# A two-layer graph network on one core: LN2's row sums and centred squares in place of bn_stats, the scale of x one group further ahead, W_O transposed between the halves of group 0's mix

## Chip, cores and metric

One core of one Trainium2 chip runs the whole program. The metric is device time in microseconds (us) of one execution; the kernel before takes 594.0 us, median of 3 runs (593.91 to 594.22). Lower is better.

## The reference

x is 128 batches of 64 nodes with 512 features; adj is one 64 x 64 matrix of zeros and ones. What is computed, cut to what matters:

```python
# layer 0
W = adj * adj
x = layernorm(x + einsum('bnf,nm->bmf', x, W) + bias)          # LN1
# layer 1
z_l = x @ W_lang.T;  z_g = x @ W_grav.T;  v = x @ W_V.T
A_l = maximum(zn @ zn.T, 0) * not_eye                          # zn: rows of z_l at norm 1
A_g = exp(-d2(z_g) / (2 * sigma**2)) * not_eye
K = w_l * rownorm(A_l * adj) + (1 - w_l) * rownorm(A_g * adj)
x = layernorm(x + (K @ v) @ W_O.T)                             # LN2
```

## The kernel before

All 128 batches are cut into 16 groups of 8. A group is 512 rows, held as 4 pairs of 128 rows (two batches each) by 512 features. There is one instruction stream for each engine, in an order written out by hand; semaphores alone tie the engines together. Float32 values enter most products as a high and a low float16 part (`h_hi`, `h_lo` and so on), three matmuls for one product. The high part is a copy on ScalarE, the low part a subtraction on VectorE, or on GpSimd for x and for two pairs of h.

`iteration(g, ...)` does, for group g, all of layer 1 up to its similarities; for `before` (g-1) the rest of layer 1 and LN2; for `nxt` (g+1) layer 0 and LN1; for `split` (g+2) the scaling of x and its split into halves. The order on TensorE in the middle of the run:

- `mix(nxt, 0)` (L420) is layer 0 for half of nxt's pairs. Its start is used below as the mark at which an iteration begins.
- `project(g, 0..3)`, then `mix(nxt, 1)`, `project(g, 4)`, `x_norm(split)` (L426, one small matmul that sums the squares of x), `kernel_t(before)` (L528), `project(g, 5)`, `attend(before, 0)` (L548), `project(g, 6)`, `attend(before, 1)`, `project(g, 7)`. The projections (L449) are 12, 9, 6, 3 matmuls of 512 columns, twice. `project(g, 0)` waits for the transposed h (`ht_hi`, `ht_lo`: eight DMA transposes per group from SyncE's queue, L345) and for `ulo_ready` of the group before, that is for `u_low` 0 and 1; `project(g, 2)` for `u_low` 3; `project(g, 3)` for `p_low(g, 0)`, `project(g, 4)` for `p_low(g, 1)`.
- `values(g, 0)`, `gram(g)` (L481), `values(g, 1..3)` (L467), `spread` (L496) and `symmetrise` (L505, L507), and the next mark.

The chain that leads to `spread`, over four engines: `gram` -> `t_copy` (ScalarE) -> `t_diagonal` (GpSimd, L1343) -> `diagonals`, `squared_norms` (VectorE) -> `inverse_norm` (GpSimd, a power, L1349, makes `rr`) -> `diagonal_matrices` (VectorE, L960, makes `r_sb`) -> `spread`. After `symmetrise`: `rectify`, `exponent` (ScalarE), `similarities`, `gravities`, `row_sums` and so on (VectorE) -> `ks_sb` -> `kernel_t`.

LN2 of the group before: `residual` (L1011, VectorE) adds h to the product and writes `o`; `out_stats` (L1016) is one bn_stats for each pair; `out_moments` (L1020, L1022) aggregates; `ln2` on GpSimd adds epsilon and takes the power -1/2; `out_shift` (L1026) makes -mean * rstd in `nmr2`; `normalise` (L748, ScalarE) scales each pair; one DMA stores the group (L323).

x of a group needs one scale (a power of the sum of its squares): `x_squares` (L686) -> `x_sum` -> `x_norm` -> `x_base` -> `x_scale` and `x_back` (GpSimd) -> `x_inverse`; `x_scaled` (L691) applies it, `x_high` (L697) and `x_low` (L1316, GpSimd) split. All of it is done for `split` in one iteration, but for the squares, which are taken one iteration earlier.

Before the iterations: products of ones that keep TensorE busy (`keep_warm`, L403), the Gram product of W_lang (L633), layer 0 of group 0 in two halves (L420), sixteen transposes of W_O (L657) into `front`, the Gram product of W_grav (L633), which needs the banks that ScalarE has copied out, and M = W_V.T W_O.T (L668), which for each bank needs `g_copied`, VectorE's copy of the W_grav product. VectorE's order there: bias, statistics, norm and low half of group 0 (`first_bias` to `h_low`, L926), then the `g_copied` copies. In iteration 0 `m_low` (L1051) makes the low half of M, which `values(g, 0)` waits for, chunk by chunk.

## Time and profile before

| | |
|---|---|
| median of 3 runs | 594.0 us |
| the profiled execution | 594.79 us, span of its instructions 593.0 us |
| mean granted TensorE clock | 0.996 |
| busy: TensorE matmul, VectorE, ScalarE, GpSimd | 96%, 88%, 60%, 38% of the span |
| chain that ended last, by engine | TensorE 67%, VectorE 11%, GpSimd 7% |

The span runs from the first instruction's start to the last one's end. Matmuls are pipelined: the row of a 512-column float16 matmul lasts 0.38 us, and the next starts 0.216 us later when nothing holds it. A busy share of 96% can therefore hide short stalls; starts are to be compared, not only the idle times in brackets.

### The profile page before, as it was taken

The numbers are of one execution on the slowest core, as the hardware profiler recorded it, in microseconds if no ns is written. First come the engines' busy times: TensorE is split into PE (matmuls) and PEld (weight loads), VectorE is DVE, ScalarE is ACT, GpSimd is POOL, SyncE is SP. The second block draws the span as 40 slices with busy tenths as digits, with TensorE's granted clock in tenths as the row PEclk, the third lists the DMA queues.
The fourth block names the chain that finished last, engine by engine and source line by source line (L and its number), as shares of the span: only waits on it lengthen the run. The fifth ranks groups of instructions, "written<-read, shape, count | busy, mean of one in ns | idle before, by whom it ended". The sixth has DMA issues, their size and how long they took to land.

```text
span 593.0 us, 14867 instructions
## 1 busy us (share of the span) xinstructions
PE 566.6 (96%) x5743; PEld 285.0 (48%) x5743; DVE 519.6 (88%) x1027; ACT 358.4 (60%) x670; POOL 223.1 (38%) x230
## 2 busy tenths in 40 slices
PE   9899899999999999999999999999999999899993
PEld 6544545445354545445454545445454545446451
DVE  1767789998999999999999999999999999997765
ACT  2576645757566675857666675857666675634532
POOL 0141524535162533526162533526162533514021
PEclk9999999999999999999999999999999999999998
DMA  9853241344525142343525142343525130314103
GB/s 253 219 116 72 45 99 20 93 105 72 141 60 152 36 130 59 72 128 71 141 60 153 35 130 59 71 129 71 141 59 154 35 107 12 68 64 74 71 2 143
DMA packets 89659, 55.21 MB, mean 93 GB/s; under 512 B 71072, under 2 KB 71072, under 8 KB 89632
## 3 DMA queue, kind: packets, MB, share of 16 engines
q1 hardware_dynamic: 89632, 54.84, 37.4%
q8 instruction: 18, 0.29, 0.2%
q14 instruction: 9, 0.07, 0.1%
HBM read 21.27 MB, written 16.78 MB: 64 GB/s over the span
## 4 chain that ended last, share of the span: by engine, by line
PE 67%; DVE 11%; POOL 7%; issue 6%; ACT 4%; SPq 2%; DMA 1%; DVEq 0%; POOLq 0%; ACTq 0%
PE proj L449 30%; PE proj L467 12%; PE front L420 3%; PE ps_t L481 3%; DVE h L921 3%; POOL h_lo L1321 3%; PE ps_v L496 3%; POOL rr L1349 3%; SPq L345 2%; PE ps_t L505 2%; PE ps_k L548 2%; PE proj L633 2%; PE front L548 2%; PE proj L668 2%; DVE p_lo L941 2%
## 5 line engine op out<-in xcount | busy, mean ns | idle before, releaser
L1316 POOL TENSOR_TENSOR x_lo<-x_in,x_hi 128x512 f16<-128x512 f32 x60 | 72.5, 1219 | 104.6 <-ACT x_hi L697 104.6
L707 ACT ACTIVATE p_hi<-proj 128x512 f16<-128x512 f32 x128 | 75.5, 592 | 51.8 <-PE proj L449 51.3
L467 PE MATMUL proj<-m_hi,ht_hi 128*64 128x512 f16 x512 | 98.6, 382 | 0.0
L467 PE MATMUL proj<-m_hi,ht_lo 128*64 128x512 f16 x512 | 97.9, 379 | 0.0
L467 PE MATMUL proj<-m_lo,ht_hi 128*64 128x512 f16 x512 | 97.9, 379 | 0.0
L941 DVE TENSOR_TENSOR p_lo<-proj,p_hi 128x512 f16<-128x512 f32 x128 | 85.4, 678 | 4.5 <-ACT p_hi L707 4.4
L701 ACT ACTIVATE h_hi<-h 128x512 f16<-128x512 f32 x64 | 39.9, 630 | 43.4 <-DVE h L921 43.4
L1300 POOL TENSOR_TENSOR ve<-mv,eps_ln 128x4 f32<-128x4 f32 x31 | 6.2, 201 | 158.1 <-DVE mv L914 142.0
L449 PE MATMUL proj<-ht_hi,l_lang_hi 128*128 128x512 f16 x160 | 60.9, 381 | 2.7 <-DMA ht_lo<-h_lo 1.3
L449 PE MATMUL proj<-ht_hi,l_grav_hi 128*128 128x512 f16 x160 | 61.3, 383 | 0.1
L449 PE MATMUL proj<-ht_hi,l_lang_lo 128*128 128x512 f16 x160 | 60.6, 379 | 0.0
L449 PE MATMUL proj<-ht_hi,l_grav_lo 128*128 128x512 f16 x160 | 60.6, 379 | 0.0
L449 PE MATMUL proj<-ht_lo,l_lang_hi 128*128 128x512 f16 x160 | 60.6, 379 | 0.0
L449 PE MATMUL proj<-ht_lo,l_grav_hi 128*128 128x512 f16 x160 | 60.6, 379 | 0.0
L712 ACT ACTIVATE uv<-proj 128x512 f16<-128x512 f32 x64 | 37.7, 590 | 34.1 <-PE proj L467 34.1
L921 DVE TENSOR_SCALAR h<-y,mv,rstd 128x512 f32<-128x512 f32 x64 | 55.9, 896 | 1.4 <-POOL rstd L1304 1.4
L1321 POOL TENSOR_TENSOR h_lo<-h,h_hi 128x512 f16<-128x512 f32 x30 | 40.7, 1357 | 34.1 <-ACT h_hi L701 34.1
L481 PEld LDWEIGHTS ps_t<-ht_hi,p_hi 128*128 128x128 f16 x512 | 44.8, 98 | 9.4 <-issue 6.9
L1349 POOL TENSOR_TENSOR rr<-nsq,minus_half 64x8 f32<-64x8 f32 x16 | 34.2, 2136 | 39.6 <-DVE nsq L951 39.4
L481 PE MATMUL ps_t<-ht_hi,p_hi 128*128 128x64 f16 x512 | 46.6, 193 | 2.4 <-DVE p_lo L941 2.1
L481 PE MATMUL ps_t<-ht_lo,p_hi 128*128 128x64 f16 x512 | 46.5, 193 | 0.0
L481 PE MATMUL ps_t<-ht_hi,p_lo 128*128 128x64 f16 x512 | 46.5, 193 | 0.0
(210 smaller groups left out, 1319.2 us busy)
## 6 DMA issues: line engine op xcount, KB each, us to landing
x_in<-in_x SPq DMA_DIRECT2D x32, 512.0 KB, 6.3
out<-o SPq DMA_DIRECT2D x15, 1024.0 KB, 4.9
w_raw_lang<-in_L_gnn_W_lang SPq DMA_DIRECT2D x4, 256.0 KB, 3.6
o<-in_L_gnn_W_O SPq DMA_DIRECT2D x1, 1024.0 KB, 10.9
w_raw_grav<-in_L_gnn_W_grav SPq DMA_DIRECT2D x4, 256.0 KB, 11.2
uv<-in_L_gnn_W_V SPq DMA_DIRECT2D x1, 1024.0 KB, 16.2
ht_hi<-h_hi SPq DMA_TRANSPOSE x64, 2.5
ht_lo<-h_lo SPq DMA_TRANSPOSE x64, 2.5
```

The lines of the kernel that those rows point to most:

```text
L449: mm = pe.matmul(proj[j % 3][:, :], a[s][:, blk(k, c), :], b[g.parity][:, k, :], start=(n == 0), stop=(n == len(passes) - 1))
L467: mm = pe.matmul(proj[j % 3][q * N:(q + 1) * N, :], a[g.parity][:, k, rows:rows + N], b[:, k, :], start=(n == 0), stop=(n == len(passes) - 1))
L481: mm = pe.matmul(ps_t[:, b * N:(b + 1) * N], a[:, c, b, :, :].rearrange("p s n -> p (s n)"), t[g.parity][:, c, b * N:(b + 1) * N], start=( ...
L548: mm = pe.matmul(banks[2 * a + q][side * N:(side + 1) * N, :], kt[half, 2 * a + side, :], u[half, 2 * a + side, :], start=(n == 0 and 2 * ...
L701: act.activation(h_hi[:, p, :], h[g.parity][:, p, :], ACT.Copy).then_inc(hhi_ready, 1)
L707: act.activation(p_hi[:, j % 4, :, j // 4, :], by_batch(proj[j % 3]), ACT.Copy).then_inc(phi_ready, 1)
L712: act.activation(u_hi[:, p, :], proj[(8 + p) % 3][:, :], ACT.Copy).then_inc(uhi_ready, 1)
L921: dve.tensor_scalar(h[g.parity][:, p, :], y[:, p, :], mv1[:, p, 0:1], rstd1[:, p:p + 1], ALU.subtract, ALU.mult).then_inc(h_ready, 1)
L941: dve.tensor_tensor(p_lo[:, j % 4, :, j // 4, :], by_batch(proj[j % 3]), p_hi[:, j % 4, :, j // 4, :], ALU.subtract).then_inc(plo_ready, 1)
L1316: pool.tensor_tensor(x_lo[:, p, :], x_in[g.parity][:, p, :], x_hi[:, p, :], ALU.subtract).then_inc(xlo_ready, 1)
L1321: pool.tensor_tensor(h_lo[:, p, :], h[g.parity][:, p, :], h_hi[:, p, :], ALU.subtract).then_inc(hlo_ready_pool, 1)
L1349: pool.tensor_tensor(rr[L, :], nsq[L, :], minus_half[L, :], ALU.pow).then_inc(rr_ready, 1)
```

## The change

LN2 of all groups but the last no longer uses bn_stats. `residual` gives the row sums too, `out_means` turns them into -mean/sqrt(512), and ScalarE's `o_squares` takes ((o - mean)/sqrt(512)) squared with its own sum as the variance. `out_shift` moves ahead of `u_low` 1 and 2 on VectorE, `normalise(before, 0)` ahead of `rectify` on ScalarE, and `u_high(g, 3)` behind `exponent`.

The squares of x, its sum, `x_norm`, `x_base`, `x_scale`, `x_back` and `x_inverse` are now for `third` (g+3), so that the scale of `split` is known when an iteration starts; its scaling and halves move to the front of the iteration. `xscale` gets two buffers. In iteration 0 the whole of both is done: `split` and then `third`.

`mix(nxt, 1)` moves from behind `project(g, 3)` to behind `project(g, 2)`. On GpSimd `t_diagonal` goes ahead of `h_low(nxt, 2)` and `inverse_norm` ahead of `h_low(nxt, 3)`. W_O's transposes go between the two halves of group 0's mix and into `weight_bank`. `WARM_START` goes from 5 to 10.

```diff
-WARM_START = 5
+WARM_START = 10
...
+                         in1=h[g.parity][:, p, :], op0=ALU.mult, op1=ALU.add,
+                         accum_out=osum[:, p:p + 1]).then_inc(sum_ready, 1)
-            def out_stats(g, p): ...
-            def out_moments(g): ...
+            def out_means(g, half):
+                pairs = slice(2 * half, 2 * half + 2)
+                dve.wait_ge(sum_ready, g.count(4, 2 * half + 2))
+                dve.tensor_scalar(omean[:, pairs], osum[:, pairs], -(D ** -1.5), None, ALU.mult).then_inc(omean_ready, 1)
...
+            def o_squares(g, p):
+                act.wait_ge(omean_ready, g.count(2, p // 2 + 1))
+                act.activation(o_square[:, p, :], o[:, p, :], ACT.Square, scale=D ** -0.5, bias=omean[:, p:p + 1],
+                               accum_out=ovar[:, p:p + 1]).then_inc(ovar_ready, 1)
...
             def ln2(g):
-                inverse_std(g, mv2_ready, mv2, ve2_ready, ve2, rstd2_ready, rstd2)
+                pool.wait_ge(ovar_ready, g.count(4, 4))
+                pool.tensor_tensor(ve2[:, :], ovar[:, :], eps_ln[:, :], ALU.add).then_inc(ve2_ready, 1)
+                pool.wait_ge(ve2_ready, g.count(1, 1))
+                pool.tensor_tensor(rstd2[:, :], ve2[:, :], minus_half[:, 0:PAIRS], ALU.pow).then_inc(rstd2_ready, 1)
```

The new order on each engine, from the values on (TensorE: `x_norm(third)` after `values(g, 1)`):

```
ScalarE, iterations with a group before and a third:
  p_high 0, x_scaled(split) 0 1, p_high 1, p_high 2, ks_high, x_high(split) 0, p_high 3, x_scaled(split) 2 3,
  kt_high, p_high 4, x_high(split) 1 2, p_high 5, x_squares(third) 0 1, p_high 6, p_high 7, x_squares(third) 2 3,
  h_high 0 1 2, o_squares 0, t_copy, x_high(split) 3, o_squares 1, u_high 0, h_high 3, o_squares 2, u_high 1,
  o_squares 3, u_high 2, normalise 0, rectify, exponent, u_high 3, normalise 1 2 3
VectorE, from p_low 5: residual 2, p_low 6, residual 3, p_low 7, out_means 0, norm_rows 0 1 2, h_low 0,
  out_means 1, x_sum(third), h_low 1, norm_rows 3, diagonals, squared_norms, x_base(third), u_low 0, shifted,
  diagonal_matrices, out_shift, u_low 1, u_low 2, x_inverse(third), similarities, gravities, add_bias 0, u_low 3
GpSimd: x_low(split) 0, ln1 with x_low(split) 1 inside, t_diagonal, h_low 2, inverse_norm, h_low 3,
  x_scale(third), x_back(third), ln2(before), x_low(split) 2 3
ScalarE, iteration 0: p_high 0, x_squares(split) 0 1, p_high 1, x_squares(split) 2 3, p_high 2, m_high 0, p_high 3,
  m_high 1, p_high 4, x_scaled(split) 0 1 2 3, p_high 5, x_squares(third) 0 1, p_high 6, p_high 7,
  x_high(split) 0 1 2, x_squares(third) 2 3, h_high 0 1 2, t_copy, ...
VectorE, iteration 0: add_bias 0, row_stats 0, add_bias 1, p_low 0, m_scale, x_sum(split), row_stats 1, p_low 1, ...
  x_base(split), row_stats 3, p_low 4, ... p_low 7, norm_rows 0 1 2, h_low 0, m_low 0 1 2 3, ...
```

```diff
             mix(Group(0, 0), 0, first=True)
+            pe.wait_ge(o_moved, 16)
+            for c in range(DC):
+                pe.wait_ge(l_copied, c + 1)
+                for e in range(DC):
+                    mm = pe.transpose(weight_bank[c][:, e * P:(e + 1) * P],
+                                      w_raw["o"][:, e, c * P:(c + 1) * P], ident[:, :])
+                mm.then_inc(wot_done, 1)
             pe.wait_ge(wssq_ready, 1)
...
             mix(Group(0, 0), 1, first=True)
-            pe.wait_ge(o_moved, 16)
-            for c in range(DC):
-                ...
-            pe.wait_ge(l_copied, DC)
             gram_of("grav")
```

## Rows read from the trace of the kernel before

**Rows 1.** Waits of TensorE, whole span: us in total, times, longest.

```profile
PE ps_v L496 <- DVE r_sb L960: 4.5, 8, 0.6
PE ps_v L496 <- issue: 3.0, 7, 0.5
...
PE proj L449 <- DMA ht_lo<-h_lo: 1.3, 2, 0.9
```

**Rows 2.** Timeline of TensorE at the marks: start us, length us, idle in brackets.

```profile
78.02 0.41 PE L420 MATMUL front<-x_hi,wmix_hi 64*64 64x512 f16 x4
...
279.60 0.41 PE L420 MATMUL front<-x_hi,wmix_hi 64*64 64x512 f16 x4
...
312.89 0.41 PE L420 MATMUL front<-x_hi,wmix_hi 64*64 64x512 f16 x4
...
513.25 0.41 PE L420 MATMUL front<-x_hi,wmix_hi 64*64 64x512 f16 x4
```

**Rows 3.** Timeline of TensorE inside the iteration that starts at 279.60.

```profile
285.99 0.38 PE L449 MATMUL proj<-ht_hi,l_lang_lo 128*128 128x512 f16 x1
286.40 0.39 PE L449 MATMUL proj<-ht_hi,l_lang_hi 128*128 128x512 f16 x1
...
299.14 0.38 PE L467 MATMUL proj<-m_hi,ht_lo 128*64 128x512 f16 x2
299.45 0.20 PE L481 MATMUL ps_t<-ht_hi,p_hi 128*128 128x64 f16 x1
...
309.93 0.38 PE L467 MATMUL proj<-m_hi,ht_lo 128*64 128x512 f16 x2
310.78 0.67 PE L496 MATMUL ps_v<-r_sb,w_spread 128*128 128x512 f32 x1 [0.47 <-issue]
```

**Rows 4.** Timeline of GpSimd, same iteration.

```profile
303.70 1.46 POOL L1343 TENSOR_TENSOR t_diag<-t_sb,eye 128x512 f32<-128x512 f32 x1
...
307.83 2.13 POOL L1349 TENSOR_TENSOR rr<-nsq,minus_half 64x8 f32<-64x8 f32 x1 [1.11 <-DVE nsq L951]
...
311.39 1.01 POOL L1304 TENSOR_TENSOR rstd<-ve,minus_half 128x4 f32<-128x4 f32 x1
```

**Rows 5.** Timeline of VectorE, same iteration: p_low 1 and the matrix for spread.

```profile
287.06 0.68 DVE L941 TENSOR_TENSOR p_lo<-proj,p_hi 128x512 f16<-128x512 f32 x1
...
310.00 0.68 DVE L960 TENSOR_TENSOR r_sb<-eye,rr 64x512 f32<-64x512 f32 x1 [0.80 <-POOL rr L1349]
```

**Rows 6.** Instructions on tile nmr: duration ns min/median/max, first and last start.

```profile
L1026 DVE SCALAR_TENSOR_TENSOR nmr<-mv,rstd x15: 154/1109/1117, 111.3 to 574.0; 128x4 f32<-128x4 f32 x15
```

**Rows 7.** Groups of instructions by line and form: busy us, mean ns | idle.

```profile
L686 ACT ACTIVATE x_square<-x_in 128x512 bf16<-128x512 f32 x60 | 37.1, 620 | 0.8 <-DMA x_in<-in_x 0.8
...
L686 ACT ACTIVATION_READ_ACCUMULATOR x_square<-x_in 128x1 f32 x60 | 11.6, 193 | 0.0
```

**Rows 8.** Timeline of TensorE before iteration 0 and at its gram.

```profile
17.04 1.09 PE L420 MATMUL front<-x_in,wmix 64*64 64x512 f32 x8
19.03 1.16 PE L657 MATMUL front<-ident,o 128*128 128x128 f32 x8 [0.91 <-DVE y L885]
...
30.01 3.60 PE L668 MATMUL proj<-wo_t,uv 128*128 128x512 f32 x8
...
62.25 0.19 PE L481 MATMUL ps_t<-ht_hi,p_hi 128*128 128x64 f16 x1 [2.10 <-DVE p_lo L941]
```

**Rows 9.** Timeline of SyncE's queue: the load of W_O.

```profile
5.84 0.43 SPq L354 DMA_DIRECT2D o<-in_L_gnn_W_O  x1
```

**Rows 10.** DMA issues by line: KB each, median us to landing.

```profile
o<-in_L_gnn_W_O SPq DMA_DIRECT2D x1, 1024.0 KB, 10.9
```

**Rows 11.** Timeline of VectorE before and in iteration 0.

```profile
25.63 2.50 DVE L926 TENSOR_TENSOR h_lo<-h,h_hi 128x512 f16<-128x512 f32 x4
...
63.23 3.63 DVE L1051 SCALAR_TENSOR_TENSOR m_lo<-m_f,up,m_hi 128x512 f16<-128x512 f32 x4
```

**Rows 12.** Timeline of ScalarE in iteration 0: two x_scaled.

```profile
58.97 1.33 ACT L691 ACTIVATE x_in<-x_in,xscale 128x512 f32<-128x512 f32 x2
```

More of the change, by code:

```diff
@@ L486, in gram, with spread @@
                 mm.then_inc(gram_done, 1)
-            def spread(g, first, split):
-                if split:
-                    pe.wait_ge(xbase_ready, split.prev().count(1, 1))
+            def spread(g, first, third):
+                if third:
+                    pe.wait_ge(xbase_ready, third.prev().count(1, 1))
                 pe.wait_ge(shifted_ready, g.count(1, 1))
@@ L574, in iteration @@
                 split = nxt.next() if has_split else None
+                third = split.next() if has_square else None
                 if has_next:
@@ L578, in iteration @@
                     mix(nxt, 0)
+                project(g, 0, first)
                 if first:
@@ L611, in iteration @@
                 if has_next:
+                    if has_square:
+                        pe.wait_ge(xsum_ready, third.prev().count(1, 1))
+                        if first:
+                            pe.wait_ge(xbase_ready, 2)
+                        x_norm(third)
                     values(g, 2)
                     values(g, 3)
-                    spread(g, first, split)
+                    spread(g, first, third)
                     symmetrise(g, split)
@@ L766, in iteration @@
                 split = nxt.next() if has_split else None
-                square = split.next() if has_square else None
-                if first:
-                    m_high(0)
+                third = split.next() if has_square else None
                 p_high(g, 0, first)
@@ L772, in iteration @@
                     x_squares(split, 0)
-                    m_high(1)
+                    x_squares(split, 1)
+                elif has_split:
+                    x_scaled(split, 0)
+                    x_scaled(split, 1)
                 p_high(g, 1, first)
-                if first:
-                    x_squares(split, 1)
-                p_high(g, 2, first)
                 if first:
@@ L1104, in iteration @@
                 split = nxt.next() if has_split else None
+                third = split.next() if has_square else None
+                if has_prev:
+                    gravities(before)
                 if has_next:
                     add_bias(nxt, 0)
-                if has_split and not first:
-                    x_sum(split)
                 if has_prev:
-                    gravities(before)
                     u_low(before, 3)
@@ L1123, in iteration @@
                 p_low(g, 0)
+                if first:
+                    m_scale()
+                    x_sum(split)
                 if has_prev:
@@ L1133, in iteration @@
                 p_low(g, 2)
-                if first:
-                    x_sum(split)
                 if has_next:
@@ L1159, in iteration @@
                     residual(before, 2, False)
+                p_low(g, 6)
+                if has_prev:
                     residual(before, 3, False)
-                p_low(g, 6)
                 p_low(g, 7)
+                if has_prev:
+                    out_means(before, 0)
                 if has_next:
                     norm_rows(nxt, 0, before)
+                    norm_rows(nxt, 1, before)
+                    norm_rows(nxt, 2, before)
+                    h_low(nxt, 0)
                 if first:
@@ L1301, in inverse_std @@
                 if between:
-                    x_scale(between)
+                    x_low(between, 1)
                 pool.wait_ge(ve_ready, g.count(1, 1))
@@ L1357, in iteration @@
                 split = g.next().next() if has_split else None
-                if has_next:
-                    ln1(nxt, split)
-                if has_split:
+                third = split.next() if has_square else None
+                if first:
+                    x_scale(split)
+                    x_back(split)
+                    ln1(nxt)
                     x_low(split, 0)
                     x_low(split, 1)
-                    x_back(split)
+                else:
+                    if has_split:
+                        x_low(split, 0)
+                    if has_next:
+                        ln1(nxt, split)
                 if has_next:
+                    t_diagonal(g)
                     h_low(nxt, 2)
-                    t_diagonal(g)
+                inverse_norm(g)
+                if has_next:
                     h_low(nxt, 3)
-                inverse_norm(g)
+                if has_square:
+                    x_scale(third)
+                    x_back(third)
                 if has_prev:
```

174 lines of the change are left out of this document (86 added, 88 removed).

## The prediction

> **What bounds the kernel now.** I read the table of busy shares first: TensorE is busy in 96% of the span, so an edit counts only by what it does to TensorE's idle time. The view of its waits comes next. The reader is to see that one stall repeats: `spread` waits for `r_sb`, named as the matrix itself or as "issue", 15 times and 7.5 us in all; the transposed h was late twice, for 1.3 us [rows 1]. Third come the marks, the starts of `mix(nxt, 0)`. From the first (78.02) to the fourteenth (513.25) are 13 periods, 33.48 us on average; one of the middle is 33.29 [rows 2]. TensorE's timeline inside it shows what the list of waits hides: its rows overlap, so that only starts tell. From the last matmul of the values to `spread` are 0.85 us, where the same kind of change of stage, values to `gram`, takes 0.31: a stall of 0.54. And within `project(g, 3)` one step takes 0.41 where 0.216 is the rule: another 0.2, for `p_low 0` [rows 3]. So a period has a floor of about 33.48 - 0.9 = 32.6; the 0.9 is 0.54 to 0.68 at `spread` (7.5 us of waits over 15, and some 0.1 of overlap each), 0.2 at the projection and the rest of the first three periods, where the transposes and `p_low` were later still.
>
> **Part 1: LN2 and the reordered tail.** VectorE loses four bn_stats (0.68 each, 0.60 from start to start) and four aggregations, and gains two tiny multiplications and the sums of the four residuals. No VectorE row shows what such a sum costs. Bounds: 0, or 0.1 a residual, which is what ScalarE's read of its accumulator adds between starts (its row of 193 ns overlaps the one before [rows 7]). I take 0.07, as for the smallest VectorE instructions; 0.3 a group. VectorE still gains some 2 us a group between `p_low 7` and `diagonals`. ScalarE gains four squares of about 0.71 from start to start (620 ns and its read [rows 7]), 2.9 us. It is busy 60% of the time, so its sum hides them; where they stand matters, below.
>
> The chain to `spread`: let Γ be the start of `gram` (299.45 [rows 3]). Before, `t_diagonal` started at Γ+4.25 behind `h_low 2`, and `inverse_norm` at Γ+8.4, held by VectorE, which was busy with statistics and `u_low 0` [rows 4]. After: `t_copy` ends at Γ+3.6 (a `gram` of 2.9, 0.1, a copy of 0.6), `t_diagonal` takes 1.46 [rows 4] and `h_low 2` 1.16, to Γ+6.2, when `diagonals` and `squared_norms` (0.95) are done as well. The power takes 2.13 [rows 4], to Γ+8.35, and `diagonal_matrices` 0.68 [rows 5], to Γ+9.05, or Γ+10.1 if it is held by `h_low 3`, which GpSimd starts at the same moment. `spread` could start at Γ+10.5 (309.93 + 0.31 - 299.45 [rows 3]) plus 0.03 for the moved `x_norm`. It no longer waits: 0.6 a period. Before, its end was 2.11 us ahead of the next mark (310.78 to 312.89 [rows 2, 3]), so the new mark is at Γ+12.95.
>
> What is late next is LN2's own chain, which the change puts in front of things that TensorE needs. GpSimd after the power: `h_low 3` to Γ+9.55, `x_scale` and `x_back` to about Γ+10.3, the addition to Γ+10.6, rstd 1.01 [rows 4] to Γ+11.6. The squares of ScalarE are done by then: the last follows the values' second part at about Γ+7.9. `out_shift` waits for rstd, and `u_low 1`, `u_low 2` and `similarities` are queued behind it; `normalise 0` waits for `out_shift`, and `rectify`, `exponent` and `u_high 3` are queued behind that.
>
> How long `out_shift` takes is the disputed price: its fifteen rows have a median of 1109 ns and a minimum of 154, on four columns [rows 6]. The long ones stand beside an `x_low` of GpSimd, the short one beside an idle GpSimd. After the change it again meets `x_low 2`, which starts as rstd ends. So 1.1, to Γ+12.7; 0.15 is the other end. The Trainium skill (SBUF — State Buffer, Who interferes with whom) states that a VectorE instruction with two SBUF inputs contends with a GpSimd instruction that reads SBUF, and that whoever is first keeps the shared pair to its end. By that rule `out_shift` always waits for the whole `x_low`, and the row's median agrees.
>
> From Γ+12.7 on: `u_low 1` ends at Γ+13.4, and `project(nxt, 0)` wants it at Γ+12.95+0.77 = Γ+13.7: 0.3 to spare. `normalise 0` takes 0.71, `rectify` 0.62 and `similarities` starts at Γ+14.2, 1.25 after the mark, where it was at 0.74 before. From there to the end of `p_low 1` stand in VectorE's queue, as starts: 0.7 similarities, 0.7 gravities, 0.65 bias, 0.6 `u_low 3`, 0.6 row sums, 0.6 statistics, 0.07, 0.65 bias, 0.15 clamp, 0.6 `p_low 0`, 0.1, 0.55 statistics, 0.15, 0.68 `p_low 1`: 6.8 us, to 8.05 after the mark (before it ended at 8.14: 287.06 + 0.68 - 279.60 [rows 2, 5]). `mix(nxt, 1)` now stands ahead of `project(g, 3)`, so `p_low 0`, at 6.65, is in time for 7.4, and the 0.2 there goes. `project(g, 4)` wants `p_low 1` at 8.03 and gets it some 0.1 late. So the period is 32.6 + 0.1; as this chain has no slack, each 0.1 more on GpSimd or ScalarE is 0.1 on the period. Bounds: 32.6 (`out_shift` at 0.15), and 33.1 (0.4 more, if `h_low 3` and `x_back` are held up by VectorE). I take 32.75. Thirteen periods: 13 x (33.48 - 32.75) = 9.5 us saved; between 4.9 and 11.4.
>
> **Part 2: the scale of x two groups ahead.** The same instructions as before, moved. GpSimd gets two `x_low` out of the way of the `norm_rows` (the tile's halves are ready earlier), the transposes of h start over 1 us earlier, and the 0.9 us that TensorE waited for them in group 14 goes [rows 1]. x of `third` is loaded when it is squared: SyncE's queue order stays, and a load is out well before `p_high 5`. In iteration 15, without mixes, `normalise 1` to `3` now hold `p_high 0` back; I charge 0.5. Tail together: -0.4.
>
> **Part 3: iteration 0.** Here both groups' x work is done at once. TensorE reaches `project(g, 0)` at about 45.7 (part 4; 46.1 before). ScalarE has four squares of `split` before `p_high 2`, and `x_sum(split)` now stands before `p_low 1` on VectorE: it waits for the last square at about 52.8, `p_low 1` ends at 54.2, and `project(g, 4)`, due at 53.4, starts at 54.3. Then `x_norm`, `x_base` and `x_scale` give the scale at 57.9, and ScalarE has four `x_scaled` (1.33 for two [rows 12], 2.5 for four) before `p_high 5` and two squares (1.4) before `p_high 6` and `7`, to 63.4; `p_low 7` ends at 64.2. `gram` starts at 64.3 instead of 62.25 [rows 8]: 2.05 lost. Then three `x_high` and two squares stand before `h_high 0` (66.9), which `h_low 0` waits for, and only behind that come the four `m_low`, 3.63 us before [rows 11]: 67.6 to about 71.2. `values(g, 0)`, due at 67.2, runs at their pace and ends at 71.9 instead of 69.8; if `t_diagonal` does not hold them up, 1.1 earlier. Lost: 1.1 to 2.1; I take 1.65. The whole: 3.7 us lost; bounds 2 and 5.
>
> **Part 4: the start.** W_O is issued at 5.84 and lands 10.9 us later, at 16.75 [rows 9, 10]. The sixteen transposes, now ahead of the second half of the mix, take about 2.3 [rows 8] from there, and the mix goes from 17.04 to about 19.35. The five further products of ones take 0.43 each and half of that is lost anyway to later work at the low clock level; they end before W_O lands, so they are hidden. VectorE's chain behind the second half moves by 2.3: its `h_low` end at 30.4 instead of 28.13 [rows 11], the first `g_copied` is at 30.8, and M starts at 30.85 instead of 30.01 [rows 8]. TensorE alone would have been ready 1.0 earlier, since 2.2 us of its waits are gone, but VectorE decides. Then M is 0.84 late, and the matmul of norms, which TensorE waited for before `project(g, 0)`, now stands behind it: 1.2 back. Net -0.4, in part 3 already.
>
> **The sum.** Against the profiled execution's 594.79 (span 593.0 and 1.8 around it): -9.5 - 0.4 + 3.7 = -6.2, so 588.6. The median of the runs is 0.8 below the profiled one: 594.0 - 6.2 = 587.8.
>
> **Rivals.** Differences within 0.2% (1.2 us) can't be told from none here.
> - *The tail chain is shorter.* `out_shift` gets through before `x_low`, or ScalarE's queue is a little faster: the period is at its floor of 32.6, and iteration 0 loses only 2 to 3. 594.0 - 11.4 - 0.4 + 2.5 = 584.7. For it speaks the 154 ns row, against it the fourteen long ones [rows 6]. Chance 0.22.
> - *The tail chain is longer.* GpSimd's small instructions are held by VectorE's: the period is 33.0 to 33.2. Then 594.0 - 5 - 0.4 + 3.7 = 592.3. Chance 0.15; a part of it counts as no change.
> - *Slower.* The one mechanism: `normalise 0` and `out_shift` wait for rstd in two in-order queues. Where rstd comes 0.6 us later than at Γ+11.6, `u_low 1` stops `project(nxt, 0)` and `p_low 1` stops `project(g, 4)`; the period is 33.35 and saves 1.7, less than iteration 0 costs: 596. It decides from a period of 33.2 on. By the Trainium skill's rule named above the price of each meeting of `h_low 3` with `diagonal_matrices` and of `x_low 2` with `out_shift` is a whole instruction; both are in the sum once, and this would need them on GpSimd's side as well. Chance 0.11.
> - *The change of statistics does nothing by itself*, since VectorE is not what TensorE waits for: then only the order counts. The sum above already says so in part: the bn_stats matter only ahead of `diagonals`. It gives the same time.
>
> The forecast itself has 0.52: periods of 32.65 to 32.95 and a loss of 3 to 4.5. Faster by over 0.2%: 0.52 + 0.22 + most of 0.15, 0.82; within 0.2%: 0.07; slower: 0.11. The range from the bounds: 13 x 0.9 and a loss of 1 to 2 give 583; a period of 33.1 and a loss of 4 give 592.7. I give 582.5 to 593.2.
>
> **What would show it right or wrong.** Marks 32.7 to 32.8 apart; `spread` 0.31 behind the last matmul of the values; a step above 0.216 before `project(g, 4)`; `out_shift` about 1.1 long and starting as rstd ends; `gram` of group 0 at 64.3, its `values(g, 0)` stretched to 4.5 us, the second mark near 81.7; M at 30.85. It is wrong if residuals with a sum take well over 0.82, if the long idle before the first `gram` (3.3 us, 2.10 before [rows 8]) is followed by matmuls at half speed, or if a store or load is late.

## The result: 589.3 us, 0.8% faster, and the profile after

Six runs of the changed kernel have a median of 589.29 us (588.82 to 589.98), six of the kernel before beside them 594.11 (593.11 to 595.71): ratio 0.9918, 95% interval 0.9903 to 0.9933. The profiled executions took 588.82 (span 587.0) and 594.79 (span 593.0). So the span lost 6.0 us where the medians lost 4.8: the profiled run of before lies 0.7 above its median, that of after 0.5 below.

The marks, from TensorE's timeline; they answer to [rows 2]:

```profile
43.73 0.41 PE L426 MATMUL front<-x_hi,wmix_hi 64*64 64x512 f16 x4
...
80.67 0.41 PE L426 MATMUL front<-x_hi,wmix_hi 64*64 64x512 f16 x4
...
277.57 0.41 PE L426 MATMUL front<-x_hi,wmix_hi 64*64 64x512 f16 x4
...
310.38 0.41 PE L426 MATMUL front<-x_hi,wmix_hi 64*64 64x512 f16 x4
...
507.05 0.41 PE L426 MATMUL front<-x_hi,wmix_hi 64*64 64x512 f16 x4
```

The period is 32.82 (310.38 - 277.57 is 32.81; before 33.29 there and 33.48 in the mean); the last of the thirteen, whose iteration has no third group and so no `x_norm`, is 32.58. From the second mark to the last 435.23 became 426.38: 8.85 saved. The second mark came 2.65 later (78.02 to 80.67): lost. From the last mark to the end of the span 79.75 became 79.95: 0.2 lost. 8.85 - 2.65 - 0.2 = 6.0, the difference of the spans.

The waits of TensorE, longest first (us in total, times, longest), against [rows 1]:

```profile
PE ps_t L487 <- DVE p_lo L970: 3.6, 2, 3.3
PE proj L676 <- DVE l_grav_f L1269: 1.5, 1, 1.5
PE proj L455 <- DMA ht_lo<-h_lo: 1.4, 2, 0.8
...
PE proj L473 <- DVE m_lo L1077: 0.6, 1, 0.6
PE proj L662 <- DMA o<-in_L_gnn_W_O: 0.5, 1, 0.5
```

`spread` is gone from the list. All that is left is at the start, in iteration 0 and in the last two iterations. Inside a period, TensorE's timeline around the moved `x_norm` (L432) and at `spread` (L502):

```profile
302.52 0.38 PE L473 MATMUL proj<-m_hi,ht_lo 128*64 128x512 f16 x2
302.84 0.18 PE L432 MATMUL ps_v<-xsum,ones 128*128 128x1 bf16 x1
302.94 0.41 PE L473 MATMUL proj<-m_hi,ht_hi 128*64 128x512 f16 x2
...
307.93 0.38 PE L473 MATMUL proj<-m_hi,ht_lo 128*64 128x512 f16 x2
308.25 1.13 PE L502 MATMUL ps_v<-r_sb,w_spread 128*128 128x512 f32 x2
```

`spread` starts 0.32 behind the last matmul of the values, where it was 0.85 [rows 3]. But from 302.52 to 302.94 are 0.42 where values follow each other every 0.216: `x_norm` costs 0.2 here. The power that `spread` hangs on, on GpSimd:

```profile
303.40 1.63 POOL L1375 TENSOR_TENSOR rr<-nsq,minus_half 64x8 f32<-64x8 f32 x1
```

It starts 6.2 behind the start of `gram` (297.22), where it was 8.4 [rows 3, 4], and takes 1.63 where it took 2.13.

LN2's chain, VectorE's timeline of the same iteration:

```profile
308.69 1.11 DVE L1052 SCALAR_TENSOR_TENSOR nmr<-omean,rstd 128x4 f32<-128x4 f32 x1 [1.96 <-POOL rstd L1354]
309.72 1.27 DVE L960 TENSOR_TENSOR uv<-proj,uv 128x512 f16<-128x512 f32 x2
...
311.16 0.68 DVE L996 TENSOR_TENSOR a_sb<-e_sb,ps_v 64x512 f32<-64x512 f32 x1
```

`out_shift` starts as rstd ends (308.65) and takes 1.11, as predicted; `u_low 1` ends at 310.4, 0.76 before `project(nxt, 0)` at 311.16; `similarities` starts 0.78 after the mark.

Iteration 0, TensorE at the gram of group 0 and in `values(g, 0)`, and the clock beside it (windows: length; busy time of each engine with its instructions in brackets; granted clock; DMA share; GB/s):

```profile
62.63 0.19 PE L487 MATMUL ps_t<-ht_hi,p_hi 128*128 128x64 f16 x1 [3.32 <-DVE p_lo L970]
...
68.77 0.38 PE L473 MATMUL proj<-m_hi,ht_lo 128*64 128x512 f16 x2
69.76 0.41 PE L473 MATMUL proj<-m_hi,ht_hi 128*64 128x512 f16 x2 [0.61 <-DVE m_lo L1077]
```

```profile
62.60:64.00 1.40, 1.37 (x42) 1.40 (x43) 1.40 (x2) 1.40 (x5) 1.40 (x2) 0.88 0.00 0
64.00:65.00 1.00, 1.00 (x23) 1.00 (x21) 1.00 (x2) 0.95 (x3) 0.70 (x1) 0.50 0.00 0
...
67.00:68.00 1.00, 1.00 (x12) 0.57 (x12) 1.00 (x3) 0.88 (x2) 0.20 (x1) 0.96 0.52 105
```

After 3.32 us of idle time and about 1 us of work the granted clock fell to 0.50, its level of 1.2 GHz, for some 3 us; gram lasted 4.38 (62.63 to 67.01) instead of 2.89. Then the last quarter of `values(g, 0)` waited for the fourth `m_low`.

### The profile page after: what moved, and what is told of

The parts are those of the page before. It is cut to its first block, busy times and chain, and to the rows that moved or that the text cites. A ratio compares the mean times of both kernels' runs of the same rounds, so it can differ in the third digit from the quotient of the medians.

```text
span 587.0 us, 14987 instructions
## 1 busy us (share of the span) xinstructions
PE 568.2 (97%) x5753; PEld 287.3 (49%) x5753; DVE 461.1 (79%) x982; ACT 396.0 (67%) x790; POOL 214.6 (37%) x230
## 4 chain that ended last, share of the span: by engine, by line
PE 85%; DVE 6%; SPq 3%; DMA 3%; ACT 2%; POOL 1%; issue 1%; POOLq 0%; DVEq 0%; ACTq 0%
PE proj L455 35%; PE proj L473 26%; PE ps_t L487 7%; PE front L426 4%; PE ps_v L502 3%; PE ps_t L511 2%; PE ps_k L552 2%; PE front L552 2%; SPq L351 2%; PE proj L676 2%; DMA o<-in_L_gnn_W_O 2%; DMA ht_lo<-h_lo 1%; PE ps_v L532 1%; DVE p_lo L970 1%; DVE h L950 1%
## 5 line engine op out<-in xcount | busy, mean ns | idle before, releaser
L1339 POOL TENSOR_TENSOR x_lo<-x_in,x_hi 128x512 f16<-128x512 f32 x60 | 76.1, 1280 | 124.4 <-ACT x_hi L705 124.4
L970 DVE TENSOR_TENSOR p_lo<-proj,p_hi 128x512 f16<-128x512 f32 x128 | 87.5, 685 | 7.2 <-ACT p_hi L715 5.6
L761 ACT ACTIVATE o<-o,nmr,rstd 128x512 f32<-128x512 f32 x60 | 45.7, 807 | 47.3 <-DVE nmr L1052 46.9
L1369 POOL TENSOR_TENSOR t_diag<-t_sb,eye 128x512 f32<-128x512 f32 x15 | 19.2, 1281 | 103.5 <-ACT t_sb L726 103.5
L487 PE MATMUL ps_t<-ht_hi,p_hi 128*128 128x64 f16 x512 | 48.1, 195 | 3.6 <-DVE p_lo L970 3.6
L487 PEld LDWEIGHTS ps_t<-ht_hi,p_hi 128*128 128x128 f16 x512 | 45.7, 99 | 10.7 <-issue 6.9
L709 ACT ACTIVATE h_hi<-h 128x512 f16<-128x512 f32 x64 | 36.8, 622 | 18.5 <-DVE h L950 18.4
L487 PE MATMUL ps_t<-ht_hi,p_lo 128*128 128x64 f16 x512 | 48.0, 195 | 0.0
L487 PE MATMUL ps_t<-ht_lo,p_hi 128*128 128x64 f16 x512 | 48.0, 195 | 0.0
L487 PEld LDWEIGHTS ps_t<-ht_lo,p_hi 128*128 128x128 f16 x512 | 45.9, 99 | 0.0
L487 PEld LDWEIGHTS ps_t<-ht_hi,p_lo 128*128 128x128 f16 x512 | 45.9, 99 | 0.0
```

Source lines behind the costliest of these rows:

```text
L487: mm = pe.matmul(ps_t[:, b * N:(b + 1) * N], a[:, c, b, :, :].rearrange("p s n -> p (s n)"), t[g.parity][:, c, b * N:(b + 1) * N], start=( ...
L709: act.activation(h_hi[:, p, :], h[g.parity][:, p, :], ACT.Copy).then_inc(hhi_ready, 1)
L761: act.activation(o[:, p, :], o[:, p, :], ACT.Identity, scale=rstd2[:, p:p + 1], bias=nmr2[:, p:p + 1]).then_inc(out_ready, 1)
L970: dve.tensor_tensor(p_lo[:, j % 4, :, j // 4, :], by_batch(proj[j % 3]), p_hi[:, j % 4, :, j // 4, :], ALU.subtract).then_inc(plo_ready, 1)
L1339: pool.tensor_tensor(x_lo[:, p, :], x_in[g.parity][:, p, :], x_hi[:, p, :], ALU.subtract).then_inc(xlo_ready, 1)
L1369: pool.tensor_tensor(by_batch(t_diag), by_batch(t_sb), over_batches(eye2), ALU.mult).then_inc(tdiag_ready, 1)
```

## Experiments

Each time is to be read beside the 594 us of the kernel before, which was run with it; ratios carry their 95% intervals. Edits are against the changed kernel unless said.

### Which half of the change carries the gain: old_statistics, only_statistics

`old_statistics` keeps every new order and puts LN2's bn_stats back, into a place where VectorE was idle:

```diff
-                    out_means(before, 0) ... out_means(before, 1)
                     h_low(nxt, 1)
                     norm_rows(nxt, 3, before)
+                    for p in range(PAIRS): out_stats(before, p)
...
                 shifted(g)
+                    out_moments(before)
```

> The changed kernel with LN2's bn_stats, aggregation and shift as before (statistics in VectorE's idle stretch of 2.5 us behind the fourth norm_rows), all the new orders kept. Theory 1, that the orders carry the gain and the bn_stats only mattered where they stood: the period stays at 32.82, spread 0.31 behind the last matmul of the values, and the time is 589.3, within 0.7 of the changed kernel's. Theory 2, that VectorE's relief carries it: diagonals come 2 us later, spread stalls again by 0.5 or more, period 33.3 to 33.5, time 594 to 597.

589.17 us, ratio 0.9911 (0.9889 to 0.9933): the changed kernel's time, and theory 1. VectorE's timeline shows the four bn_stats in the idle stretch:

```profile
298.85 2.46 DVE L1035 BATCH_NORM_STATS2 stats<-o 128x6 f32<-128x512 f32 x4
301.58 0.69 DVE L966 TENSOR_REDUCE diag<-t_diag 128x8 f32<-128x512 f32 x1 [0.26 <-POOL t_diag L1360]
```

The period is 32.81 with the old statistics (marks at 276.93 and 309.74 in TensorE's timeline). `only_statistics` is the reverse: the kernel before, with LN2's sums and squares and nothing else (squares on ScalarE ahead of and behind `t_copy`, and around `u_high 1`).

> The kernel before with only LN2's statistics changed (sums in the residual, squares on ScalarE), every order as before. Theory 1, that the four bn_stats and aggregations held diagonals back: diagonals run as t_diagonal ends, the power starts at 7 instead of 8.4 us behind the start of gram, spread waits no more, the period falls by 0.6 to 32.9 and the time to about 586, as iteration 0 loses nothing. Theory 2, that the new orders are what is needed (GpSimd's h_low ahead of the power): the stall at spread stays above 0.3, time 592 to 594.

591.47 us (586.55 to 592.51, wider than any other), ratio 0.9930 (0.9904 to 0.9957). The time is neither theory's, but the steady period is about what theory 1 said (32.9):

```profile
278.15 0.41 PE L426 MATMUL front<-x_hi,wmix_hi 64*64 64x512 f16 x4
...
284.55 0.38 PE L455 MATMUL proj<-ht_hi,l_lang_lo 128*128 128x512 f16 x1
284.96 0.39 PE L455 MATMUL proj<-ht_hi,l_lang_hi 128*128 128x512 f16 x1
...
310.94 0.41 PE L426 MATMUL front<-x_hi,wmix_hi 64*64 64x512 f16 x4
```

32.79: `spread` waits no more (308.81, 0.32 behind the values' last at 308.49); `diagonals` runs as `t_diagonal` ends and the power starts 7.2 behind the start of `gram` (305.22 - 298.01), not 8.4. The step of 0.41 for `p_low 0`, which the old place of `mix(nxt, 1)` leaves, is still there; the new orders remove that 0.2, but their place for `x_norm` costs as much, so that both halves come to the same period. What spoils the time lies outside. The first three periods are 33.2 to 33.7, the fifth 33.1, and the transposed h is late at both ends of the run (view of waits: 4.6 us, four times, against 1.4 in the changed kernel). The longest such wait (2.50) was followed by a low clock, as was the idle time before the gram of group 0:

```profile
62.10:66.60 4.50, 4.49 (x98) 4.45 (x100) 4.50 (x5) 0.69 (x2) 2.68 (x3) 0.62 0.14 29
...
541.00:543.00 2.00, 0.00 (x0) 0.00 (x0) 1.73 (x3) 1.95 (x4) 0.00 (x0) 1.00 0.00 0
543.00:545.00 2.00, 1.96 (x7) 0.83 (x8) 1.26 (x4) 1.84 (x3) 0.00 (x0) 0.70 0.00 0
```

The ten runs differ with their mean granted clock: the four longest (592.24 to 592.51, the profiled one among them) had 0.986 or 0.987, the two shortest (586.55 and 587.21) 0.996 and 0.995. At that higher clock the statistics alone, in the old orders, are faster than the whole change.

So each half of the change alone removes the stall at `spread`: the new statistics free VectorE ahead of `diagonals`, the new orders let the chain start sooner on GpSimd and find VectorE idle. Done both, the second adds nothing to the period.

### Iteration 0: first_scalar_only, first_both, first_filler

`first_scalar_only` mends ScalarE's order in iteration 0:

```diff
                 if first:
-                    for p in range(PAIRS):
-                        x_scaled(split, p)
+                    x_scaled(split, 0)
+                    x_scaled(split, 1)
                 p_high(g, 5, first)
-                x_squares(third, 0); x_squares(third, 1)
+                x_scaled(split, 2)
                 p_high(g, 6, first)
                 p_high(g, 7, first)
+                x_scaled(split, 3)
                 x_high(split, 0) ... x_high(split, 2)
-                x_squares(third, 2); x_squares(third, 3)
+                x_squares(third, 0) ... x_squares(third, 3)
```

> The changed kernel with ScalarE's order of iteration 0 mended alone: two x_scaled ahead of p_high 5, one behind it, the fourth and all squares of third behind p_high 7. Theory 1, that in iteration 0 two things are late, the products' high halves and then m_low: gram of group 0 starts at about 60.7 instead of 62.63 and keeps the full clock, but the fourth m_low still ends at 69.2 or later, so the second mark moves by 0.5 at most (80.2 to 80.7) and the time is 589. Theory 2, that the late gram and the clock behind it are what iteration 0 lost: the second mark moves by 2 to 3.5 and the time is 586 to 587.

589.25 us, ratio 0.9917 (0.9890 to 0.9943). Theory 1 was right on what decides, but the second mark, at 81.51, is 0.8 beyond its range.

```profile
60.76 0.19 PE L487 MATMUL ps_t<-ht_hi,p_hi 128*128 128x64 f16 x1 [1.50 <-DVE p_lo L977]
...
66.56 0.41 PE L473 MATMUL proj<-m_hi,ht_hi 128*64 128x512 f16 x2 [2.84 <-DVE m_lo L1084]
```

```profile
65.05 0.69 DVE L962 TENSOR_TENSOR h_lo<-h,h_hi 128x512 f16<-128x512 f32 x1 [2.24 <-ACT h_hi L709]
65.66 4.65 DVE L1084 SCALAR_TENSOR_TENSOR m_lo<-m_f,up,m_hi 128x512 f16<-128x512 f32 x4
```

The gram came 1.9 earlier, at full clock, and TensorE then stood idle for 2.84 before `m_low`. The four `m_low` took 4.65 instead of 3.75: the earlier gram brought GpSimd's `t_diagonal` and `h_low 2` forward, from 67.80 to 66.62, so that they ran beside all of the last three. In the profile of `no_x_norm` (below), where `t_diagonal` came only at 69.23, the four took 2.73. The Trainium skill (SBUF — State Buffer, Who interferes with whom) states that a VectorE instruction with two SBUF inputs contends with a GpSimd instruction that reads SBUF; these rows agree.

`first_both` also moves the cause of the second wait, in iteration 0 alone. Not shown: there `h_high` 1 and 2 and the last two squares of `third` go behind `t_copy`, `x_sum(third)` behind `squared_norms` and `x_base(third)` behind `shifted`.

```diff
+                if first: m_low(0)                      # behind row_moments(nxt)
...
                 p_low(g, 7)
+                m_low(1); m_low(2)
                 norm_rows(nxt, 0, before)
                 norm_rows(nxt, 1, before)
+                m_low(3)
                 norm_rows(nxt, 2, before)
                 h_low(nxt, 0)
-                for k in range(DC): m_low(k)
```

> The same, and in iteration 0 VectorE's m_low 0 in its idle time ahead of p_low 5, m_low 1 and 2 right behind p_low 7, m_low 3 behind norm_rows 1, with the last two squares of third behind t_copy. Theory 1: both late things are gone, gram starts at 60.7 with an idle time under 1.5 us and lasts 2.9, values(0) follow without a stop, the second mark is at about 76.3 (80.67 in the changed kernel), the periods stay 32.82, and the time is 585.0. Theory 2, that something else bounds the second mark (x_low 3 of split, which ended at 79.3, or the spread chain): 78.5 to 80, time 587 to 589.

585.85 us, ratio 0.9849 (0.9824 to 0.9874). The gram started at 60.78 at full clock and values(g, 0) and values(g, 1) ran without a stop; the second mark was at 77.84, not 76.3, in good part for a reason in neither theory. TensorE's timeline has it:

```profile
70.29 0.18 PE L432 MATMUL ps_v<-xsum,ones 128*128 128x1 bf16 x1 [1.25 <-DVE xsum L936]
```

I had put `x_sum(third)` behind `squared_norms`, where it came 3 us after its squares.

`first_filler` asks what the low clock itself had cost:

```diff
                 if first:
+                    pe.wait_ge(norm_copied, 3)
+                    keep_warm(12)
                     gram(g, first)
```

> The changed kernel with twelve products of ones on TensorE in iteration 0 between project 7 and the gram of group 0, in its idle 3.3 us; their result is read by nobody. Theory 1, that m_low decides the end of values(g, 0): the granted clock stays at full speed, gram lasts 2.9 instead of 4.4 us, but the last third of the fourth m_low still ends at 69.7, the second mark stays at 80.6 to 80.8 and the time at 589.3. Theory 2, that the fallen clock cost its 1.5 us: the second mark at 79.2, the time 587.8. Theory 3, that the clock fell for another reason than the idle time: it falls all the same.

589.48 us, ratio 0.9933 (0.9916 to 0.9951). The clock stayed at 1.00, its level of 2.4 GHz, and gram kept TensorE busy for 2.96, but the second mark was at 81.70, 1.0 later (the first was already 0.15 later):

```profile
62.77 0.19 PE L487 MATMUL ps_t<-ht_hi,p_hi 128*128 128x64 f16 x1 [0.63 <-DVE p_lo L972]
...
66.99 0.41 PE L473 MATMUL proj<-m_hi,ht_hi 128*64 128x512 f16 x2 [1.26 <-DVE m_lo L1079]
```

```profile
66.10 4.64 DVE L1079 SCALAR_TENSOR_TENSOR m_lo<-m_f,up,m_hi 128x512 f16<-128x512 f32 x4
```

The slow gram had cost nothing in the changed kernel's profile: it ended at 67.01, and `values(g, 0)` was held by the fourth `m_low` in any case. Made fast, it set GpSimd against `m_low` again. Theory 2 falls; theory 3 too, as the filled idle time is followed by no fall. But what a fall costs depends on how long it lasts. Six profiles have the same orders and 3.3 us of idle time here, and the clock fell in all six. In five gram took 4.2 to 4.45 us, and first and second mark are 36.92 to 36.94 apart; in `no_x_norm` the clock was 0.50 until 69, gram took 5.21, no `m_low` held TensorE, and the marks are 37.32 apart: there the fall cost 0.4.

### The rival with two queues behind rstd: ln2_late

```diff
-                if has_prev:
-                    ln2(before)
                 if has_split:
                     x_low(split, 2)
+                if has_prev:
+                    ln2(before)
+                if has_split:
                     x_low(split, 3)
```

> The changed kernel with LN2's two GpSimd instructions one x_low further back (behind x_low 2 of split), so that rstd comes about 1.15 us later than 308.65 in a period that starts at 277.57. It is the rival of the prediction in which two queues wait for rstd. Theory 1, that these chains have the slack read in the new trace (0.76 us before project(nxt, 0), 0.5 before project 4): u_low 1 ends 0.45 too late for project(nxt, 0), p_low 1 another 0.2 too late for project 4, the period is 33.4 to 33.5 instead of 32.82, and the time 597 to 598, slower than before. Theory 2, that nothing hangs on it: 32.82 and 589.3.

595.49 us, ratio 1.0033 (1.0020 to 1.0046): slower than before by 0.3%; the mechanism is theory 1's, the cost smaller. TensorE's timeline:

```profile
279.43 0.41 PE L426 MATMUL front<-x_hi,wmix_hi 64*64 64x512 f16 x4
...
280.61 0.39 PE L455 MATMUL proj<-ht_hi,l_lang_hi 128*128 128x512 f16 x1 [0.33 <-DVE uv L960]
...
312.83 0.41 PE L426 MATMUL front<-x_hi,wmix_hi 64*64 64x512 f16 x4
```

The period is 33.40: 0.40 behind the mark, for `u_low 1`, and 0.16 at `project(g, 4)`, for `p_low 1` (288.13 instead of 0.216 behind 287.75). So the mechanism of the rival is real. Counted from the start of `gram`, rstd ended 1.1 us later (12.54 against 11.43), of which 0.58 reach the period: it begins to cost some 0.5 behind the changed kernel's own rstd, if beyond that all of a delay arrives (estimate). Twelve periods of 0.58 more (the first was still 32.81) make 7.0 and 596.3; the range given took 0.65 and thirteen.

### The moved matmul: no_x_norm

```diff
-                        x_norm(third)          # iterations from 1 on
...
+                dve.tensor_scalar(xbase[:, :], ones[:, 0:1], 262144.0, X_NORM ** -2,
+                                  ALU.mult, ALU.mult).then_inc(xbase_ready, 1)
```

> The changed kernel without the small matmul x_norm in all iterations but the first; x_base gets a fixed number (the sum of squares that data of unit variance have) in its place, so the scale of x isn't computed from x. Theory 1, that the matmul between values 1 and 2 costs 0.2 (steps 2.71 and 0.11 where 2.6 is the rule): the period falls from 32.82 to 32.60, the time to 586.5. Theory 2, that it costs its own start-to-start time and the change of stage is there anyway: 32.75 to 32.80, 588.5 to 589.

The kernel of this run leaves out the scale's dependence on x. 585.95 us, ratio 0.9861 (0.9846 to 0.9876). Theory 1. Eight of the thirteen periods behind the second mark are 32.58 or 32.59, the others 32.64 to 32.70.

### The start: warm_five, wo_late

`warm_five` sets `WARM_START` back to 5. `wo_late` moves the block of W_O's transposes from between the halves of group 0's mix to behind the second half.

> The changed kernel with five instead of ten products of ones at the start. Theory 1, that they are hidden because the clock rises sooner behind ten of them: the Gram product of W_lang starts near 3.4 instead of 5.5 us and runs its first quarter at the low clock, both end at 14.2 to 14.3, the first mark is at 43.6 to 43.8 and the time 589.3 within 0.5. Theory 2, that they keep the product waiting and cost part of their 2.1 us: it ends at 13 to 13.5, the mark is up to 1 us earlier.

587.67 us, ratio 0.9895 (0.9869 to 0.9920); first mark at 42.98 instead of 43.73. But the five products are not the cause. The second quarter of the W_lang product started at 6.01 (7.72 in the changed kernel), so the product ended 1.7 earlier; then TensorE waited 1.47 for W_O, which by chance landed 0.74 earlier in this execution:

```profile
15.39 0.33 PE L662 MATMUL proj<-ident,o 128*128 128x128 f32 x1 [1.47 <-DMA o<-in_L_gnn_W_O]
```

So the 0.75 at the first mark is W_O's earlier landing, and the time that the shorter start gave went into the wait for it. Most of the rest lies at the end: the profiled spans differ by 2.3, of which 0.76 stand at the second mark and 1.5 behind the last, where this execution, alone among the thirteen, has no wait for the transposed h.

> The changed kernel with W_O's transposes behind the second half of group 0's mix, ahead of the Gram product of W_grav, still into the weight banks. Theory 1, as in part 4 of the prediction, that the early transposes push VectorE's chain behind the second mix half: without them that chain starts 1.3 to 2 us earlier, and as the Gram product of W_grav waits for ScalarE's copies, it ends at 28 to 29; M starts at 28.5 to 29.3 instead of 29.6, the first mark 0.3 to 1 us earlier, the time 588.3 to 589. Theory 2, that the transposes behind the mix wait for ScalarE's copies and TensorE decides: M at 30 or later, first mark 0.4 or more later, 589.7 to 590.5.

588.50 us, ratio 0.9911 (0.9884 to 0.9938), a time whose runs (587.77 to 589.90) overlap those of the changed kernel; the traces tell more. The W_lang product ended late here (the next row starts at 14.92; 14.29 in the changed kernel) and M started early all the same:

```profile
14.92 0.27 PE L654 MATMUL ps_v<-eye_l,mask 128*64 128x64 f32 x1
...
29.20 0.64 PE L676 MATMUL proj<-wo_t,uv 128*128 128x512 f32 x1
```

From the end of that product to M are 14.28 us against 15.29 in the changed kernel (14.29 to 29.58, the last 1.51 a wait for `g_copied`). The early place of W_O costs 1.0 there, but over half of that is the 0.50 that TensorE waited for W_O in that execution. In three profiles with the early place and no such wait (`first_both`, `first_filler`, `ln2_late`) the same distance is 14.71 to 14.72, which leaves 0.44 for the order itself. The late place hides a late landing as well. Theory 1 holds.

### The version that the runs point to: combined, combined_five

```diff
                     values(g, 0)
+                    x_norm(third)              # iterations from 1 on; x_sum(third) ahead of norm_rows 0
                     gram(g, first)
...
-            for p in range(PAIRS): h_low(g0, p)
+            h_low(g0, 0); h_low(g0, 1)
             for k in range(DC): ...            # the copies of the W_grav product
+            h_low(g0, 2); h_low(g0, 3)
```

These edits stand on top of `first_both`, with its `x_sum(third)` ahead of `norm_rows 3` in iteration 0.

> The version that the runs so far point to: first_both, with x_sum(third) ahead of norm_rows 3 in iteration 0 (there x_norm waited 1.25 us for it), from iteration 1 on x_sum(third) ahead of norm_rows 0 and x_norm(third) between values(g, 0) and gram, where the change of stage costs 0.1 anyway, and at the start the copies of the W_grav product ahead of h_low 2 and 3 of group 0. Theory 1: M starts at 28.2 instead of 29.6 and the first mark is at 42.4, the second 32.9 later (34.15 in first_both), periods of 32.60: together 1.3 + 1.25 + 13 x 0.22 less than 585.85, that is 580.4. Theory 2, that x_norm costs 0.2 wherever it stands and the squares come too late for gram: periods of 32.8 to 33.0, 583 to 586.

580.94 us, ratio 0.9786 (0.9772 to 0.9801), 0.5 above theory 1's figure. TensorE's timeline: M, first and second mark, and `x_norm` in its new place, 0.03 ahead of gram:

```profile
27.80 0.67 PE L678 MATMUL proj<-wo_t,uv 128*128 128x512 f32 x1 [0.30 <-DVE l_grav_f L1292]
...
42.31 0.41 PE L426 MATMUL front<-x_hi,wmix_hi 64*64 64x512 f16 x4
...
75.14 0.41 PE L426 MATMUL front<-x_hi,wmix_hi 64*64 64x512 f16 x4
...
290.29 0.38 PE L473 MATMUL proj<-m_hi,ht_lo 128*64 128x512 f16 x2
290.61 0.18 PE L432 MATMUL ps_v<-xsum,ones 128*128 128x1 bf16 x1
290.64 0.19 PE L487 MATMUL ps_t<-ht_hi,p_hi 128*128 128x64 f16 x1
```

The periods are 32.61, three of them 32.68 or 32.69. The same with five products of ones:

> The combined version with five instead of ten products of ones. In nine profiles with ten of them the second quarter of the W_lang Gram product starts at 6.90 to 8.44 us, in two with five of them at 6.01 and 7.64: the clock rises at another moment in each execution. Theory 1, that five products cost nothing in the mean and gain where the clock rises early: that quarter starts at 6.0 to 7.7, M is ready up to 0.8 earlier, 580.2 to 580.9. Theory 2, that ten are needed: it starts at 7.6 or later, 581 or more.

579.43 us (579.26 to 580.19), ratio 0.9757 (0.9741 to 0.9774), the fastest of all; the quarter started at 7.27, inside theory 1's range, and the first mark at 42.17 was 0.14 earlier.

## Why the prediction held, and where its steps did not

The prediction said 587.8; the median is 1.5 above it, inside the range, and on the side of "faster". Term by term, on the profiled spans:

| | predicted | measured |
|---|---|---|
| thirteen periods | -9.5 | -8.85 |
| iteration 0 and start | +3.7 | +2.65 |
| tail | -0.4 | +0.2 |
| sum | -6.2 | -6.0 |

That the sums agree to 0.2 is luck: each term is off by 0.6 to 1.1, and the errors cancel. The loss of 2.65 lies below the 3 to 4.5 that the forecast's own case asked for. The other 1.3 of the 1.5 is mostly scatter: the two profiled executions lie on opposite sides of their medians (0.7 and 0.5), so that the medians saved only 4.8.

**The floor.** 33.48 less the stalls gave 32.6. `no_x_norm` has periods of 32.59, `combined` of 32.61, and the changed kernel's own last one is 32.58: right to 0.02.

**The period, 32.75 predicted, 32.82 measured: two mis-sized terms that cancel, again by luck.** `x_norm` between `values` 1 and 2 was charged 0.03 and costs 0.22 (32.81 against 32.59 without it). And LN2's chain was charged 0.1 to 0.15 for `p_low 1`, "as this chain has no slack"; it has. `similarities` started 0.78 after the mark, not 1.25: rstd ended at 308.65, where Γ+11.6 gave 308.8 (the power had ended 0.5 sooner than charged, but most of that was lost again up to rstd); `normalise 0` and `rectify` took what was charged, but I had put `similarities` at Γ+14.2 where their sum gives Γ+14.0, and the mark itself came 0.2 later by `x_norm`. So `p_low 1` ended 7.53 after the mark, not 8.05. VectorE's row, one period earlier:

```profile
284.42 0.68 DVE L970 TENSOR_TENSOR p_lo<-proj,p_hi 128x512 f16<-128x512 f32 x1
```

`ln2_late` measured what was free: 1.1 us of delay cost 0.58. The step that expected a step above 0.216 before `project(g, 4)` is wrong, those on `spread` and on `out_shift` (1.11, as rstd ends) are right. The slower rival was put at rstd 0.6 behind Γ+11.6 and a period of 33.35; `ln2_late` had it at 0.94 behind and 33.40, so the rival was real and priced some 0.3 us too steep. Two slips of the working change nothing: 309.93 + 0.31 - 299.45 is 10.8, not 10.5, and the mark at Γ+12.95 goes with 10.8; and the 2.11 us ahead of the next mark (310.78 to 312.89) run from the start of `spread`, not from its end.

**The residual's sum.** Charged 0.07 each. Residuals 0 and 1 start 0.67 apart (291.82, 292.49), before 0.66 (294.05, 294.71): 0.01.

**The statistics.** "The change of statistics does nothing by itself" is half right. Given the new orders they do nothing (`old_statistics`). But the reason given, that VectorE is not what TensorE waits for, is wrong in the old order: there they alone take the period to 32.79, as the prediction's own aside (they "matter only ahead of `diagonals`") allows. The two halves of the change do the same job twice.

**Iteration 0, 3.7 lost predicted, 2.65 measured.** The gram was put at 64.3 and came at 62.63. 1.2 of the 1.7 is the start, below (`project(g, 0)` at 44.50, not 45.7); the rest is that four squares of ScalarE were done at 51.2, 0.4 sooner than that explains, so that `p_low 1` held `project(g, 4)` less. Then `values(g, 0)` was put to m_low's pace from its start and sized 4.5; it took 3.4 (67.01 to 70.43), as only the fourth `m_low` held it. Where `m_low` was not moved it decided (`first_scalar_only`, `first_filler`). The cause I priced highest, the late gram, decided nothing by itself: with it repaired by 1.9 us the second mark came 0.8 later, not sooner. Both repaired, and the 1.25 of `x_sum` as well (`combined`), put the second mark 32.83 behind the first instead of 36.94: 4.1 us less, and 1.1 less than in the kernel before (33.94).

**The clock.** The prediction named matmuls at half speed behind the long idle as a thing that would make it wrong. They came (4.38 for 2.89) and cost nothing, for m_low would have held TensorE anyway; in `no_x_norm`, where they lasted longer, they cost 0.4. An event on the busiest engine is worth what it moves at the next point where engines meet.

**The start.** M was put at 30.85 and came at 29.58. The transposes were sized 2.3, from rows in which they wait for `front` to be copied out; into four banks of their own they took 1.8 (16.13 to 17.94), and W_O landed 0.7 sooner. But the direction of the step, that VectorE's chain decides and TensorE's shorter waits are worth nothing, was right: TensorE waited 1.51 for `g_copied`, and against `wo_late` the early place loses 1.0, or 0.44 where W_O is there in time.

**The tail.** -0.4 predicted, +0.2 measured. The wait for the transposed h did not go: 0.69 in group 14 and 0.76 in group 15.

## What to carry to other kernels

A stall between two engines can often be removed from either side; price the second remedy with the first one in place, for it may be worth nothing (here both did, alone, all of it) and still cost something elsewhere, as the long iteration 0 did. Where a matmul of one column has to go somewhere, put it where the stage changes anyway (0.03) and not inside a run of equal products (0.22). When an engine's idle time is repaired, look for who is next late at the same meeting point, and for whom the earlier finish brings into contention, before counting the gain.

## What the hardware showed that was not expected

**The clock falls behind the same idle time in one execution and not in another.** With 2.10 us of idle time before the gram of group 0, the granted clock stayed at 1.00 in the kernel before (gram 2.89) and was 0.62 over the gram in `only_statistics` (4.4 us). 3.3 (the changed kernel and five others), 2.84 (`first_scalar_only`, 0.50 from 68 to 70) and 2.50 (above) were followed by a fall, 1.50 in `first_both` and `combined` by none. One kernel alone shows the chance: of seventeen runs of the kernel before, beside `old_statistics`, four granted 0.989 in the mean and took 595.55 to 596.61, the other thirteen 0.995 to 0.997 and 592.99 to 594.77. Where the clock fell in those four is not known.

**The start scatters by more than the edits made there are worth.** In nine profiles with ten products of ones the second quarter of the W_lang product started between 6.90 and 8.44 us, in four with five between 6.01 and 7.64 (means 7.7 and 6.8); W_O, always issued at 5.84 to 5.86, landed between 14.5 and 16.8. Whichever is later starts the transposes: in the changed kernel's profile it was W_O, and ten products cost nothing; in `first_filler` the product, and they cost up to 1.6 (estimate: 8.44 against the mean of 6.8). The profiles' clock column reads 1.00 over the whole start; that the matmuls are slow there is read from their lengths. A quarter of the product takes 2.16 from start to start at full speed, and the first one took 2.16 to 2.96 behind ten products of ones, 2.65 to 4.26 behind five. The Trainium skill (TensorE: Matmul & The Clock Gate, Part 1: The HAM clock gate (the "warmup" mystery)) states that the moment at which the clock rises varies from run to run; these profiles agree. Whether five or ten is better by more than 0.5 us stays open: `combined_five` is 1.5 faster than `combined` and their profiled spans differ by 1.6, but of that the first mark has only 0.14; 1.2 is the wait for the transposed h at the end (0.2 against 1.4).

**Transposes are slower in the last iterations.** SyncE's queue in `only_statistics`, group 15:

```profile
529.34 3.02 SPq L351 DMA_TRANSPOSE ht_lo<-h_lo  x1
532.41 1.27 SPq L351 DMA_TRANSPOSE ht_hi<-h_hi  x1
```

In the periods of the middle each takes 1.27 in the queue; in the last ones some take 1.6 to 3.0, and in all profiles but that of `warm_five` TensorE waits for the transposed h there, for 0.2 to 1.6 us in all and 2.5 in `only_statistics`. The DMA queues for instructions move packets in those stretches (2 and 3 in the 15 us or so around the transposes of groups 14 and 15, none in the same stretch of a middle period). Those iterations are written out behind the loop. That the one causes the other was not tried.
